# Order and seeding of the transposed score groups in a fused attention and mixture-of-experts kernel, and one early load

## What is computed

```python
Q, K, V = proj(layernorm(x)), proj(ctx), proj(ctx)           # 16 heads of 8
scores = einsum('bhid,bhjd->bhij', Q, K) / sqrt(8) + slope[h] * softplus(1000 + abs(i - j))
x = x + (softmax(scores) @ V) @ Wo.T + bo
xf = layernorm(x)
probs = softmax(xf @ Wr); topk_p, topk_i = top_k(probs, 2)   # 16 experts, two for each token
x = x + sum_e cw_e * (silu(xf @ Wg_e) * (xf @ Wu_e)) @ Wd_e + shared(xf)
```

## Time and profile before

| | us |
|---|---|
| median of 3 runs (lowest, highest) | 237.85 (237.54, 238.19) |
| the profiled execution | 236.51 |
| its span, first to last instruction | 234.7 |
| PE busy | 214.3 (91%) |
| PEld busy | 175.2 (75%) |
| DVE busy | 175.5 (75%) |
| ACT busy | 118.9 (51%) |
| POOL busy | 74.3 (32%) |

### The profile page before, as it was taken

One profiled execution on the slowest core, in us unless ns is written; L12 is line 12 of the kernel. 1 busy time (PEld: TensorE's weight loads), 2 busy tenths in 40 slices (PEclk: granted clock), 3 DMA queues, 4 the chain that ended last, 5 costly groups with the idle time before them and its releaser, 6 DMA issues.

```text
span 234.7 us, 6077 instructions
## 1 busy us (share of the span) xinstructions
PE 214.3 (91%) x1938; PEld 175.2 (75%) x1938; DVE 175.5 (75%) x612; ACT 118.9 (51%) x283; POOL 74.3 (32%) x178
## 2 busy tenths in 40 slices
PE   2979866979999999999999999999999899989995
PEld 2757444757888777977897888878887679768884
DVE  4589526995799678985899569967885788654891
ACT  8566645376336734474346543663367334763310
POOL 2520007010770159012931095107800580037000
DMA  5653488245113350327042701452134500350000
GB/s 158 173 89 105 102 155 270 73 93 140 43 35 81 117 128 0 106 52 201 0 102 49 188 13 56 92 135 68 34 87 104 135 0 4 78 131 0 1 25 22
DMA packets 13079, 20.24 MB, mean 86 GB/s; under 512 B 2800, under 2 KB 9440, under 8 KB 12544
## 3 DMA queue, kind: packets, MB, share of 16 engines
q1 hardware_dynamic: 12624, 18.77, 31.9%
q10 hardware_dynamic: 432, 1.19, 1.7%
HBM read 16.03 MB, written 3.78 MB: 84 GB/s over the span
## 4 chain that ended last, share of the span: by engine, by line
PE 41%; issue 33%; DVE 10%; POOL 9%; ACT 3%; DMA 1%; DVEq 0%; POOLq 0%; SPq 0%; ACTq 0%
PE ps_up L525 8%; PE ps_m L553 8%; PE ps_pv L458 4%; PE ps_st L439 4%; PE ps_up L530 4%; DVE nmax L977 4%; POOL hid L1324 3%; PE ps_pv L465 3%; DVE tg L1081 2%; DMA ident<-in_c_ident 1%; PE ps_s L381 1%; PE ps_m L480 1%; POOL xb L1306 1%; PE ps_st L486 1%; PE ps_st L493 1%
## 5 line engine op out<-in xcount | busy, mean ns | idle before, releaser
L801 ACT ACTIVATE th<-ps_up 128x256 f32<-128x256 f32 x72 | 27.6, 384 | 39.1 <-PE ps_up L530 38.6
L553 PE MATMUL ps_m<-wd_sb,hid 128*128 128x128 f32 x288 | 44.8, 283 | 0.2 <-DVE hid L1223 0.2
L977 DVE TENSOR_REDUCE nmax<-ps_s 128x4 f32<-128x512 f32 x64 | 42.1, 682 | 1.4 <-PE ps_s L381 0.8
L749 ACT ACTIVATE probs<-ps_st 128x512 f32<-128x512 f32 x64 | 36.8, 592 | 11.2 <-PE ps_st L439 10.9
L1081 DVE SCALAR_TENSOR_TENSOR tg<-th,ps_up 128x256 f32<-128x256 f32 x72 | 29.8, 414 | 13.2 <-ACT th L801 12.9
L553 PEld LDWEIGHTS ps_m<-wd_sb,hid 128*128 128x128 f32 x288 | 37.5, 191 | 1.4 <-DVE hid L1223 0.4
L1324 POOL TENSOR_TENSOR hid<-hid,crep 128x256 f32<-128x256 f32 x54 | 37.7, 730 | 0.2 <-issue 0.2
L1087 DVE TENSOR_TENSOR hid<-tg,ps_up 128x256 f32<-128x256 f32 x72 | 29.8, 413 | 1.0
L525 PE MATMUL ps_up<-x_hi,wg_hi 128*128 128x256 f32 x72 | 26.6, 369 | 0.4 <-ACT x_hi L782 0.2
L439 PE MATMUL ps_st<-stacks_sb 98*128 98x128 f16 x256 | 24.9, 220 | 0.4 <-DMA stacks_sb<-nmT 0.3
L1288 POOL TENSOR_TENSOR ve<-mv,eps_sb 128x1 f32<-128x1 f32 x16 | 3.1, 191 | 69.2 <-DVE mv L1028 69.2
(11 more groups left out here) (148 smaller groups left out, 433.7 us busy)
## 6 DMA issues: line engine op xcount, KB each, us to landing
crep<-cw_dram SPq DMA_DIRECT2D x28, 256.0 KB, 4.5
stacks_sb<-qk_dram SPq DMA_DIRECT2D x32, 128.0 KB, 3.3
qk_dram<-qk_parts SPq DMA_DIRECT2D x16, 128.0 KB, 1.8
out_y<-x_all SPq DMA_DIRECT2D x8, 128.0 KB, 4.2
wg_sb<-in_wgT ACTq DMA_DIRECT2D x1, 576.0 KB, 4.1
wu_sb<-in_wuT ACTq DMA_DIRECT2D x1, 576.0 KB, 3.4
wd_sb<-in_wd SPq DMA_DIRECT2D x1, 576.0 KB, 4.0
x_all<-in_x SPq DMA_DIRECT2D x2, 256.0 KB, 4.2
```

Of the source, the lines that this page charges most:

```text
L553: last = mm(ps_dn[:, b * P:(b + 1) * P], hid[:, buf, c, b * P:(b + 1) * P], wd_sb[:, c, :], start=(c == 0 and b == 0), stop=(c == SHARED), ...
L749: fn(probs[:, b, g * HG * P:(g + 1) * HG * P], scores_bank(a, g)[:], ACT.Exp).then_inc(exp_sb, 1)
L801: fn(th[:, c % 2, :], ps_up[c % 2][:, 0, :], ACT.Tanh, scale=0.5).then_inc(tanh_sb, 1)
L977: v.tensor_reduce(nmax[:, b, HG * g:HG * g + HG], ps_s[g % 2][:].rearrange("p (h j) -> p h j", h=HG), AX_X, ALU.max, negate=True).then_inc ...
```

## The change

`ORDER = (0, 3, 1, 2)` says which group is computed at which place i = 0 to 3 of a half; banks go by the place. Group 1 of the first half is now seeded too, by ScalarE in `seed_second`, right behind the first exponential of the half, whose bank it fills. In the second half DVE's seed of group 1 fills the bank that the first exponential of that half has read, so it waits for that one, and `gate(f, 5)` and `hidden(f, 5)` stand ahead of it, `norm1(q)` behind. The load of x for pairs 2 and 3 moves ahead of step 0 on SP and waits for the stacks of pair 0.

```diff
+ORDER = (0, 3, 1, 2)
@@ load_more
-                sp.dma_start(x_all[:, 2 * NB:4 * NB, :], x[:, 2 * NB:4 * NB, :]).then_inc(s_x, 16)
                 sp.dma_start(ctx_all[:, 2 * T:4 * T], ctxT[:, 2 * T:4 * T]).then_inc(s_ctx, 16)
@@ SP, at the start
             stack_q(0, 0)
+            sp.wait_ge(s_stack, 64)
+            sp.dma_start(x_all[:, 2 * NB:4 * NB, :], x[:, 2 * NB:4 * NB, :]).then_inc(s_x, 16)
             step(None, 0, 1, 2, 0)
@@ TensorE
-            def scores_T(a, b, g, buf, f=None):
-                bank, n = scores_bank(a, g), 2 * NHG * a + NHG * b + g
-                seeded = not at_start(a) and (b, g) in ((0, 0), (1, 0), (1, 1))
+            def scores_T(a, b, i, buf, f=None):
+                g, bank, n = ORDER[i], scores_bank(a, i), 2 * NHG * a + NHG * b + i
+                seeded = not at_start(a) and g < 2
                 if seeded and b == 0:
-                    pe.wait_ge(seed0_sb, a)
+                    pe.wait_ge(seed0_sb, 2 * a + g - 1)
                 elif seeded:
                     pe.wait_ge(seed1_sb, 2 * a + g - 1)
-                elif not (at_start(a) and b == 0 and g < 2):
+                elif not (at_start(a) and b == 0 and i < 2):
                     pe.wait_ge(exp_sb, n - 1)
-                if g == 0:
+                if i == 0:
                     pe.wait_ge(s_nm[b], 16 * a + 16)
@@ ScalarE
-            def exponential(a, b, g):
-                act.wait_ge(st_mm, 2 * NHG * a + NHG * b + g + 1)
+            def exponential(a, b, i):
+                g = ORDER[i]
+                act.wait_ge(st_mm, 2 * NHG * a + NHG * b + i + 1)
...
+            def seed_second(a):
+                act.wait_ge(exp_sb, 2 * NHG * a + 1)
+                fn(ps_st[1][:], bias_T[:, 1, :], ACT.Copy).then_inc(seed0_sb, 1)
@@ ScalarE, step
                 exponential(a, 0, 0)
+                seed_second(a)
                 shift_copy(a, 1)
@@ VectorE
             def seed(a, g):
-                dve.wait_ge(exp_sb, 2 * NHG * a + NHG + g - 1)
-                v.tensor_copy(ps_st[(g + 1) % 2][:], bias_T[:, g, :]).then_inc(seed1_sb, 1)
+                dve.wait_ge(exp_sb, 2 * NHG * a + NHG - 1 + 2 * g)
+                v.tensor_copy(ps_st[1][:], bias_T[:, g, :]).then_inc(seed1_sb, 1)
@@ VectorE, second_half
                 hidden(f, 4, 1 - abuf)
                 seed(a, 0)
+                gate(f, 5)
+                hidden(f, 5, 1 - abuf)
                 seed(a, 1)
-                gate(f, 5)
                 if q is not None: norm1(q)
-                hidden(f, 5, 1 - abuf)
                 if not at_start(f): residual2(f - 1)
                 row_sums(a, 0)
```

More of the change, by code:

```diff
@@ L415, in bias_tiles @@
                     last.then_inc(bias_mm, 1)
-            def scores_T(a, b, g, buf, f=None):
-                bank, n = scores_bank(a, g), 2 * NHG * a + NHG * b + g
-                seeded = not at_start(a) and (b, g) in ((0, 0), (1, 0), (1, 1))
+            def scores_T(a, b, i, buf, f=None):
+                g, bank, n = ORDER[i], scores_bank(a, i), 2 * NHG * a + NHG * b + i
+                seeded = not at_start(a) and g < 2
                 if f is not None:
                     pe.wait_ge(lsh_sb, f + 1)
-                if at_start(a) and (b, g) == (0, 1):
+                if at_start(a) and (b, i) == (0, 1):
                     pe.wait_ge(qklo_sb, 4)
                 if seeded and b == 0:
-                    pe.wait_ge(seed0_sb, a)
+                    pe.wait_ge(seed0_sb, 2 * a + g - 1)
                 elif seeded:
                     pe.wait_ge(seed1_sb, 2 * a + g - 1)
-                elif not (at_start(a) and b == 0 and g < 2):
+                elif not (at_start(a) and b == 0 and i < 2):
                     pe.wait_ge(exp_sb, n - 1)
-                if g == 0:
+                if i == 0:
                     pe.wait_ge(s_nm[b], 16 * a + 16)
@@ L743, in shift_copy @@
                 fn(nmT[:, b, :], ps_nm, ACT.Copy).then_inc(nm_sb, 1)
-            def exponential(a, b, g):
-                act.wait_ge(st_mm, 2 * NHG * a + NHG * b + g + 1)
-                if g == 0 and not at_start(a):
+            def exponential(a, b, i):
+                g = ORDER[i]
+                act.wait_ge(st_mm, 2 * NHG * a + NHG * b + i + 1)
+                if i == 0 and not at_start(a):
                     act.wait_ge(pv_mm, 2 * a + b - 1)
-                fn(probs[:, b, g * HG * P:(g + 1) * HG * P], scores_bank(a, g)[:], ACT.Exp).then_inc(exp_sb, 1)
+                fn(probs[:, b, g * HG * P:(g + 1) * HG * P], scores_bank(a, i)[:], ACT.Exp).then_inc(exp_sb, 1)
             def seed_first(a, p):
```

## The result

The changed kernel took 239.95 us (median of 7 runs, 237.39 to 240.49) where the kernel before took 237.33 beside it (7 runs, 236.45 to 238.19): ratio 1.010, 95% interval 1.006 to 1.014. So it is slower, by 0.65 to 1.0%.

What follows compares the result with a forecast made beforehand. DVE was taken to bound each step up to `cw`, with TensorE's work counting only behind `weights_T`. Steps +1.63 and the early x load -0.7 gave +0.93 us, so 238.8 us (+0.4%), range 237.1 to 239.9.

Steps and rivals of the forecast that it cites:

- What bounds the kernel: DVE bounds each pipeline turn up to `cw`, for which `weights_T` waits; behind it TensorE runs without a gap.
- The faster rival: The wait at `weights_T` gives way, so TensorE's removed work counts everywhere: 235.6 us, chance 0.15.
- idle of 0.5 to 0.8 ahead of L501: Expected sign in steps 1 to 5: TensorE idles 0.5 to 0.8 us before `weights_T`, still starting 0.05 after `cw`.
- the whole 0.54: Bias matmuls of groups 1 and 2 taken from ahead of `weights_T`: 0.54 us relief, buying nothing in steps 1 to 5.
- The two terms behind `weights_T`: Group 2's bias matmul in fourth place of each half: 0.16 us each, +0.32 a step.
- The seed in the third place: Second half, DVE's seed of group 1 ends 0.25 later than worked out and becomes the path: 240.2 us, chance 0.12.
- `seed_second`: New 128x512 copy on ScalarE between first exponential and `shift_copy`: cost 0, at most 0.6 us a step.
- The overlap of ScalarE: At `seed_second`, the 93 ns overlap of successive ACTIVATEs would be lost once, 0.09 us a step, but idle time covers it.
- The steps' sum: Seven pipeline turns: +0.41 in step 1, +0.32 in each of 2 to 5, +0.16 in 6, -0.22 in 7; +1.63 us.
- The start: Early x load ends DVE's 3.71 us wait; ScalarE's wait for `wd` comes next, so -0.7 us, at most -1.3.
- the Trainium skill's rule on queues: DMA engines alternate between queues per packet, so early x delays `wu` by its own transfer, hidden under ScalarE's 2.12 us idle.
- The forecast of +0.4%: Whole kernel: +0.93 us, giving 238.8 us against a base of 237.85; chance 0.40 with its own range 238.3 to 239.4.

Runs made afterwards that it cites:

- the relief alone: Kernel before with three bias matmuls fewer ahead of `weights_T` (first half's groups in order 0, 2, 1, 3), second half unchanged, x load late: 237.26 us, ratio 1.002.
- the trace without the two disturbances: Profile of the changed kernel with 12 unread transposes on TensorE ahead of the first `expert_in_T`: median 238.47 us, ratio 1.004, 236.71 at full clock.
- both loads early: Loads of x and `wd` both issued early; in the kernel before with nothing else changed: 234.85 us, ratio 0.989.
- the third experiment: Changed kernel with 12 unread transposes in TensorE's idle time ahead of the first `expert_in_T`: 238.47 us, ratio 1.004.

## Why the prediction came out as it did

**What bounds the kernel** held. `weights_T` waits for `cw` in steps 1 to 5 at the same distance (but for step 3 where SP's issue was long), DVE's stretch is the same, and the relief alone is worth nothing (237.26 against 237.29). The faster rival, that the wait at L501 gives way, is refuted by that run and by the timelines. That DVE's queue had no gap to close was right, but it had work in it that could go behind `cw`, 0.27 a step, which I had not looked for. I had said idle of 0.5 to 0.8 ahead of L501; steps 2 to 5 show 0.36 there, and step 1 0.79 at full clock. I had let the whole 0.54 arrive at L501 and missed TensorE's earlier wait for DVE, at `shift_T`, which takes 0.2 of it.

**The two terms behind `weights_T`** held to 0.02: `values_T` 4.2, `weigh_values(a, 1)` +0.31, the halves separately 0.15 and 0.16. The seed in the third place did not become the path: it ends at 157.08, and `values_T` waits for ScalarE's copy, which ends at 157.39. **`seed_second`** cost nothing. The overlap of ScalarE that the prediction weighed against it shows: the exponential ends at 151.17, the seed starts at 151.20, and `shift_copy` behind the seed starts 0.07 before that ends. The Trainium skill's rule (ScalarE: Activation LUTs, What ACT_TABLE_LOAD costs), an overlap of about 0.093, so agrees in kind with the 0.07 here, and its loss is hidden as forecast.

**The steps' sum**, +1.63, measured +1.37 in the trace without the two disturbances: 0.12 too much in step 6, where in before TensorE's lateness of 0.16 had grown to 0.26 by `weigh_values`, 0.08 in steps 2 to 5 together, and 0.05 in step 1. **The start**, -0.7, measured -0.62 in after, -0.85 at full clock with the load alone; `wd` was next, as named. `wu` was delayed as the Trainium skill's rule on queues (DMA: Bandwidth & Descriptors, Queues, rings and completion order) had it: it landed after 4.8 us instead of 3.4 (4.9 with the load alone early, 3.3 with the order alone changed), and ScalarE's idle ahead of the second `shift_copy` shrank from 2.12 to 1.58. That is hidden, as forecast.

**What was missing** are two terms of the sum, not its mechanism. At full clock the changed kernel is 1.2 to 1.4 us slower (237.39 and 237.79 against 236.19 and 236.36), where the sum had 0.93; 0.4 to 0.6 of it is SP's long issue in step 6: I had walked through SP's queue for the moved load but took the time of an issue as fixed. The other is TensorE's clock. The prediction read PE's idle time ahead of L501 as costing nothing, and in time it does; but after's fallen clock cost 1.9 in its profile, and its executions were at full clock in 1 of 7 and 6 of 12. How often it falls differs between kernels: in 18 of 18 executions with both loads early and under 0.65 us of idle at each wait in step 1 it stayed full, in 12 of 24 with 0.75 and 0.8 it did not. Before has short idles there too, but 2.14 and 0.39 at the start, x early alone 1.50 (full in 8 of 12), and before loses about 1 us on the mean that way. In the profiles in which it fell, it fell at 35.7 to 41.6 us in five, in or behind the idles at the start, and at 50.1 in the changed kernel with `wd` early, behind those of step 1. That idle time ahead of the fall is the cause is a reading that fits these kernels, and it isn't shown: the third experiment, which filled an idle at the start and changed nothing else, kept full clock no more often (5 of 12), and no run took away the two idles of step 1 alone. What makes one execution fall and the next not stays open. The Trainium skill (TensorE: Matmul & The Clock Gate, A second HAM failure mode) says of another kernel that frequent short idles between groups of matmuls make the clock go to and fro. These rows agree in that no idle of TensorE's behind the first 18 us and ahead of a fall was longer than 2.1 us; to and fro they don't show, for between its rise at the start and the last microseconds the clock fell once at most in a profile.

Last, the level: I took the median of three runs, 237.85, as the base. With more runs it was 237.0 to 237.4. The forecast of +0.4% was low by 0.25 to 0.6 of a per cent, and 238.8 came near the second median partly for that base.

## What to carry to other kernels

Ask of each instruction that is moved on which side of the next wait it falls: 0.54 us of matmuls removed ahead of a wait for another engine gave nothing, and 0.16 put behind it cost all of itself, twice a step. Where two engines arrive within 0.2 us of each other, shorten both in one edit (VectorE's stats behind `cw` gave 0.25 a step with the relief, 0.04 to 0.13 without). And before taking work from a TensorE that waits, look at how long it then sits idle, for its clock may fall; a load that is next in line (`wd`) won 0.8 us at the start, where the reordering won nothing.

## What the hardware showed that I had not expected

- TensorE's clock fell to half, for 3 to 10 us in the profiles, in many executions of the same kernel, before included (76 of 91 below full on their mean). It took 1.9 us in the profile of after; between the executions of one kernel that kept full clock and those that didn't the means differ by 0.9 to 2.1.
- A DMA issue on SP that takes 0.39 or 0.46 us elsewhere took 1.12 to 1.68 in step 6 beside a 16 KB packet of program code, in all seven kernels that have 21 matmuls less and no idle transposes, and in none of the others. Twelve instructions more on TensorE moved the packet 1.6 to 1.7 us ahead, and the issue was 0.46 again, in two kernels. All 18 issues over 1.0 us in the traces end 0.35 to 0.40 after such a packet does.
- A cast of 128x16 on VectorE took 0.17 us in most places, and 0.74 to 0.81 where a product of GpSimd ran beside it; it then ended 0.03 after the product.
